# AdaLN block on one core: the B matrices by batch in column groups, with the loads at a stage's start in another order

## The reference

```python
logits = _rms(x, norm_pre_w) @ compete_w.T + compete_b        # 16 slots per batch
vals, idx = top_k(swapaxes(logits, 1, 2), 4)
wgt = softmax(vals, axis=-1)
wx = x @ write_w.T + write_b
gathered = take_along_axis(wx[:, None], idx[..., None], axis=2)
written = einsum('bsk,bskd->bsd', wgt, gathered)
ws = _rms(ws + written, norm_post_w)
q  = (x @ wq.T + bq).reshape(B, L, H, 64)                     # H = 16 heads
kk = (ws @ wk.T + bk).reshape(B, S, H, 64)
vv = (ws @ wv.T + bv).reshape(B, S, H, 64)
att = softmax(einsum('blhd,bshd->bhls', q, kk) / 8, axis=-1)
ctx = einsum('bhls,bshd->blhd', att, vv).reshape(B, L, 1024)
x = _rms(x + ctx @ out_proj_w.T + out_proj_b, norm_post_w)
```

## Time and profile before

| | |
|---|---|
| median of 3 runs | 1112.16 us (1110.51 to 1112.85) |
| profiled execution | 1110.51 us, span 1108.7 us |
| PE busy | 1022.6 us (92%) |
| PEld busy | 579.1 us (52%) |
| DVE busy | 763.4 us (69%) |
| ACT busy | 590.7 us (53%) |
| POOL busy | 459.3 us (41%) |
| DMA | 232.38 MB, mean 210 GB/s |

### The profile page before, as it was taken

How to read it: one execution, slowest core, us unless ns; L and a number is a source line. 1 busy time by engine, 2 the same in 40 slices (tenths; PEclk the granted TensorE clock), 3 DMA queues, 4 the chain that set the end, 5 groups by cost and what they waited for, 6 DMA issues and landing times. The chain is left out here.

```text
span 1108.7 us, 14369 instructions
## 1 busy us (share of the span) xinstructions
PE 1022.6 (92%) x4784; PEld 579.1 (52%) x4784; DVE 763.4 (69%) x1024; ACT 590.7 (53%) x977; POOL 459.3 (41%) x212
## 2 busy tenths in 40 slices
PE   2999999999999968989999999998789899999996
PEld 1344444444444432746666666665327566666663
DVE  4999999999999922365555555554315666666664
ACT  3778878878788630245555555556204333333333
POOL 6899899899999620001111111111100033333333
PEclk9999999999999998999999999999699999999998
DMA  4356555565555469954556576443797666868664
GB/s 137 133 181 199 171 182 179 176 203 163 183 186 171 133 209 411 338 171 158 184 195 229 187 232 213 171 171 127 268 409 279 189 208 215 298 222 294 231 227 151
DMA packets 122143, 232.38 MB, mean 210 GB/s; under 512 B 8163, under 2 KB 83043, under 8 KB 119013
## 3 DMA queue, kind: packets, MB, share of 16 engines
q1 hardware_dynamic: 121444, 229.54, 60.1%
q0 software_dynamic: 640, 2.10, 0.6%
HBM read 139.32 MB, written 92.28 MB: 209 GB/s over the span
## 5 line engine op out<-in xcount | busy, mean ns | idle before, releaser
L966 PE MATMUL bank<-work 128*128 128x256 f32 (+1 forms) x1024 | 244.4, 382 | 8.1 <-PEq L555 5.0
L995 PE MATMUL bank<-work 128*128 128x512 f32 (+1 forms) x512 | 230.3, 592 | 2.1 <-ACT work L1097 1.3
L416 PE MATMUL bank<-work,ident 128*128 128x512 f32 x384 | 190.9, 620 | 40.3 <-DVE work L338 39.6
L966 PEld LDWEIGHTS bank<-work 128*128 128x128 f32 x1024 | 187.2, 190 | 45.2 <-issue 25.3
L1157 POOL TENSOR_TENSOR work<-work 128x1024 f32<-128x1024 f32 x32 | 75.5, 2359 | 237.3 <-DVE work L1079 237.3
L1147 POOL COPY xres<-work 128x1024 f32<-128x1024 f32 x32 | 33.4, 1043 | 332.7 <-DVE work L1079 332.7
L995 PEld LDWEIGHTS bank<-work 128*128 128x128 f32 x512 | 97.1, 190 | 97.6 <-issue 91.8
L416 PEld LDWEIGHTS bank<-work,ident 128*128 128x128 f32 x384 | 65.9, 190 | 146.4 <-issue 99.2
L1030 DVE TENSOR_TENSOR work<-bank,sbias 128x256 f32<-128x256 f32 x64 | 27.2, 424 | 151.4 <-PE bank L966 151.4
L416 PE MATMUL bank<-work 128*128 128x511 f32 x256 | 121.1, 596 | 0.0
L330 DVE SCALAR_TENSOR_TENSOR work<-work,decay 128x512 f32<-128x512 f32 x128 | 120.7, 962 | 0.0
(11 more groups left out here) (153 smaller groups left out, 1437.5 us busy)
## 6 DMA issues: line engine op xcount, KB each, us to landing
work<-in_kT SPq DMA_DIRECT2D x32, 512.0 KB, 3.3
work<-in_xT SPq DMA_DIRECT2D x32, 512.0 KB, 3.9
x0T_scratch<-work SPq DMA_DIRECT2D x32, 512.0 KB, 3.5
x_natural_scratch<-xres SPq DMA_DIRECT2D x32, 512.0 KB, 5.0
work<-x0T_scratch SPq DMA_DIRECT2D x32, 512.0 KB, 4.3
x_natural_scratch<-work SPq DMA_DIRECT2D x32, 512.0 KB, 3.0
x1T_scratch<-work SPq DMA_DIRECT2D x32, 512.0 KB, 2.7
work<-x1T_scratch SPq DMA_DIRECT2D x32, 512.0 KB, 4.9
```

What stands on the lines that cost most here:

```text
L416: return nc.tensor.matmul(ps[:, at:at + n], w, v, start=start, stop=not start, skip_group_check=True)
L966: last = nc.tensor.matmul(ps_s[p], xTb[p][:, c, :], Amat[:, i, :, c * 32:c * 32 + 32], start=(c == 0), stop=(c == NC - 1))
L995: last = nc.tensor.matmul(ps_o[:, cols], attT[:, k * P:(k + 1) * P], Bmat[k][:, i, cols], start=(k == 0), stop=(k == 1), skip_group_check= ...
```

## The change

Everything is in the head, but for the names of the semaphores that the tail waits for.

- B by batch. There are 8 groups, one for each half k of the heads and each batch b, in the order of `groups`. A group has 4 pairs of heads, whose 32 rows go to the 4 column groups of the array (8 matmuls with outputs of 32 rows by 512 columns, one for each pair and half of the columns). The rows come out where `Bmat` and `Bm_d` have them, so a group is evicted in one instruction of 128 x 1024. VectorE evicts groups 0 to 3 and ScalarE groups 4 to 7.
- The output bias is added as VectorE evicts groups 0 to 3 (the first half of the heads), from a buffer `obias` in which 16 rows hold the bias and the rest is zero. GpSimd clears it behind its gathers. The matmuls with K = 1 and their row vectors `head0_row` are gone.
- TensorE starts the groups when VectorE has evicted product 7. Groups 0 and 4 each wait for two quarters of wo_T. A group waits for the eviction of the group three before it, whose bank it takes. Groups (0,2), (0,3) and (1,3) share one staging buffer, so group 3 waits for the write of group 0, and group 5 for that of group 3.
- The 8 score-bias matmuls go to four column groups, in two sets, with one copy of 128 x 256.
- SP sends both wr_T pieces first. Then it waits for the last gather, and sends the write bias and the workspace, the first wk_T piece, the norm weights and the output bias.

```diff
-            step(nc.vector.memset(head0_row[0], 0.0))
...
+        stageB = {(0, 2): cut(8192, 1024), (0, 3): cut(8192, 1024), (1, 2): cut(2048, 1024), (1, 3): cut(8192, 1024)}
+        groups = [(0, 2), (0, 0), (0, 1), (0, 3), (1, 2), (1, 3), (1, 0), (1, 1)]
...
                     piece(0, wr_T, 0)
+                    piece(1, wr_T, 1)
+                    sp.wait_ge(g_in[K - 1], 16)
+                    for h in range(2):
+                        half = slice(CH * h, CH * h + CH)
+                        sp.dma_start(wbb[64 * h:64 * h + 64, :], wr_b[half].rearrange("(o c) -> o c", o=1)
+                                     .broadcast_to([BS, CH])).then_inc(c_in, 16)
+                        if t == 0:
+                            sp.dma_start(ws[64 * h:64 * h + 64, :], work_t[:, half]).then_inc(c_in, 16)
+                    piece(2, wk_T, 0)
                     if t == 0:
...
-                    sp.wait_ge(g_in[K - 1], 16)
-                    piece(1, wr_T, 1)
-                    piece(2, wk_T, 0)
+                        sp.dma_start(npb, npost.rearrange("(o c) -> o c", o=1).broadcast_to([P, C])).then_inc(np_in, 16)
+                    sp.wait_ge(ob_zero, 1)
+                    sp.dma_start(obias[0:S, :], wo_b.rearrange("(o c) -> o c", o=1).broadcast_to([S, C])).then_inc(ob_in, 16)
...
+                    for g, (k, b) in enumerate(groups):
+                        if b >= 2:
+                            wait_group(sp, g)
+                            sp.dma_start(Bm_d[b, k, :, :], stageB[k, b]).then_inc(b_out[t][k, b], 16)
+                        if g == 3:
                             load_bias(sp, t, 1)
+                            sp.wait_ge(grp_ps, 4)
                             load_x(sp, t, 0, 0, 0, 0)
...
-                        r0 = 32 * (hp // 4)
-                        last = nc.tensor.matmul(psK[r0:r0 + 1, hp % 4 * P:(hp % 4 + 1) * P], bqc[:, hp:hp + 1],
-                                                kkz[:, hp, :, :], start=True, stop=True)
+                        r0 = 32 * (hp % 4)
+                        last = nc.tensor.matmul(psK[r0:r0 + 1, hp // 4 * P:(hp // 4 + 1) * P], bqc[:, hp:hp + 1],
+                                                kkz[:, hp, :, :], start=True, stop=True, skip_group_check=True)
...
+                    pe.wait_ge(vv_ok, 4)
+                    pe.wait_ge(sb_ok, 1)
+                    wait_product(pe, HP - 1)
+                    for g, (k, b) in enumerate(groups):
+                        if g % 4 == 0:
+                            for i in range(2):
+                                pe.wait_ge(wo_in[2 * k + i], 16)
+                        wait_group(pe, g - 3)
+                        for h in range(2):
+                            cols = slice(CH * h, CH * h + CH)
+                            for j in range(4):
+                                last = nc.tensor.matmul(group_bank(g)[32 * j:32 * j + 32, cols],
+                                                        vvz[:, 4 * k + j, b, :], ring[k][:, j, cols],
+                                                        start=True, stop=True, skip_group_check=True)
+                        last.then_inc(grp_ps, 1)
+                    wait_product(pe, HP - 2)
+                    keep_warm(banks[0], 3)
...
+                    nc.gpsimd.memset(obias[:], 0.0).then_inc(ob_zero, 1)
...
+                    for g in range(4, 8):
+                        nc.scalar.activation(group_home(act, g), group_bank(g)[:, :], ACT.Copy).then_inc(grp_a, 1)
...
+                    dve.wait_ge(ob_in, 16)
+                    for g in range(4):
+                        nc.vector.tensor_tensor(group_home(dve, g), group_bank(g)[:, :], obias[:], ALU.add)\
+                            .then_inc(grp_d, 1)
```

More of the change, by code:

```diff
@@ L82, in build @@
         rows = sb("rows", [P, P])
[L83 removed]
+        ones_row = rows[0:1, :]
         tiny = sb("tiny", [P, 4])
@@ L510, in load_x @@
             sp.dma_start(xTb[p], src).then_inc(xT_in[t][p], 16)
-        b_out = [[sem(f"B_out_{t}_{i}") for i in range(4)] for t in range(2)]
-        def slot_of(i):
-            k = i - HP
-            return (k % 2, k // 2) if k < 6 else (k % 4, 0)
+        b_out = [{g: sem(f"B_out_{t}_{g[0]}_{g[1]}") for g in stageB} for t in range(2)]
         def head(t):
@@ L540, in prod, with wait_product, group_bank, wait_group @@
             def prod(i):
[L542 to L544 removed]
+                return banks[(0, 3)[i % 2]]
+            def wait_product(eng, i):
                 if i >= 0:
[L547 to L548 removed]
+                    eng.wait_ge(ev_d if i % 2 else ev_a, 2 * (i // 2 + 1))
+            def group_bank(g):
+                return banks[1 + g % 3]
+            def wait_group(eng, g):
+                if g >= 4:
+                    eng.wait_ge(grp_a, g - 3)
+                elif g >= 0:
+                    eng.wait_ge(grp_d, g + 1)
             def keep_warm(ps, n):
@@ L703, in _ @@
-                    wait_product(pe, 2 * HP - 4)
-                    keep_warm(prod(2 * HP - 4), 3)
+                    for hp in range(HP):
+                        ps = prod(hp)
+                        wait_product(pe, hp - 2)
+                        if hp % 4 == 0:
+                            pe.wait_ge(w_in[hp // 4], 16 * 3)
+                        for c in range(NC):
+                            last = nc.tensor.matmul(ps[:, c * P:(c + 1) * P],
+                                                    ring[hp // 4][:, hp % 4, c * P:(c + 1) * P], kkz[:, hp, :, :],
+                                                    start=True, stop=True)
+                        last.then_inc(prod_ps, 1)
@@ L709, in copy_product, with group_home @@
                     done, ps = ev_d if i % 2 else ev_a, prod(i)
[L710 to L729 removed]
+                    new = ps[:, :].rearrange("p (c b r) -> p b c r", c=NC, b=B)
+                    copy(Amat[:, :, i, :].rearrange("p b (c r) -> p b c r", c=NC), new[:, 0:2, :, :])\
+                        .then_inc(done, 1)
+                    wait(eng, st_a[i % 4], 16 * (i // 4))
+                    copy(stageA[i % 4].rearrange("p (b c r) -> p b c r", b=2, c=NC), new[:, 2:B, :, :])\
+                        .then_inc(done, 1)
+                def group_home(eng, g):
+                    k, b = groups[g]
+                    eng.wait_ge(grp_ps, g + 1)
+                    if b < 2:
+                        if k == 0:
+                            for j in (2 * b, 2 * b + 1):
+                                eng.wait_ge(st_a[j], 16 * 2)
+                        return Bmat[k][:, b, :]
+                    if (k, b) == (0, 3):
+                        eng.wait_ge(b_out[t][0, 2], 16)
+                    if (k, b) == (1, 3):
+                        eng.wait_ge(b_out[t][0, 3], 16)
+                    return stageB[k, b]
                 @block.gpsimd
@@ L870, in wait_Bm @@
             def wait_Bm(eng):
-                for k in range(4):
-                    eng.wait_ge(b_out[t][k], 32 * (3, 3, 1, 1)[k])
+                for g in b_out[t]:
+                    eng.wait_ge(b_out[t][g], 16)
             ps_s = [banks[0][:, 0:256], banks[0][:, 512:768]]
```

100 lines of the change are left out of this document (16 added, 84 removed).

## The result

The changed kernel takes 1115.55 us (median of 12 runs, 1112.32 to 1117.08) beside 1112.1 us for the kernel before on the same chip: a ratio of 1.0029, interval 1.0018 to 1.0041. It is slower by 0.3%, where 1102.7 us was forecast. The profiled execution took 1115.01 us with a span of 1113.1 us, 4.4 us more than before.

The account below looks back on a forecast made before the run. PE was taken as busy nearly throughout except in the two heads. Gains of 4.1 (first head) and 4.15 (second) made 8.25 us off 1110.5, 1102.2, set 0.5 higher at 1102.7 us; range 1097.5 to 1108.5, likeliest case 1100 to 1105.

Parts of the forecast that it names:

- 4.15: Second head's loads: the 2.45 us wait for wv_T and 1.7 us of slow clock both go.
- The gathers' delay: Second head: the second wr_T piece goes before the gathers, so PE's transposes come 3.8 us later (ends 0 and 4.4).
- the score bias: Each head: products in four column groups let the transposes start earlier, gain 0.4 us (ends 0 and 1.1).
- The 1.7 us of slow clock: Second head, behind the wait for wv_T: 32 matmuls taking 5.34 us return to 3.64.
- I take a gain of 2.4: First head's loads: the stream is 2.4 us shorter, leaving some 0.3 of PE's 2.74 us of waits.
- The last write lands at 865.3: Second head's B stage: last B write lands then, next tile's load at 868.7, before PE's own end at 869.7.
- Forecast gains 1.6 and 3.4: B stage: us gained in the first and second head, the first after 0.6 taken off for the clock.
- the free biases at the write product: Write bias and workspace loads behind the gathers cost nothing, covered by the 10.04 us write product.
- rival 3: B groups: four column groups with different moving operands don't run together, 3.6 us a group, time 1128; chance 0.04.
- Rival 1: Loads: gathers share the engines with the second piece, delayed 0.5 instead of 3.8 us, time 1099.4; chance 0.14.
- Rival 2: B stage: a falling clock takes its gain, -1.1 and 0.0 for 1.6 and 3.4, time 1108.8 (half: 1105); chance 0.20.
- The premise that a tail keeps whatever it gains at its start: Tails: an earlier start is kept in full, since PE has no gaps inside a tail.

Follow-up runs that it names:

- order_only: The kernel before with only the changed kernel's new order of loads: 1114.66 us, ratio 1.0024.
- wr_half: The changed kernel with the second wr_T piece cut to half its columns, leaving out part of the computation: 1112.43 us, one run.
- groups_only: The changed kernel with the order of loads of before, keeping the B groups and score bias: 1111.13 us, ratio 1.0003.
- mixed: no_warm with the second wr_T piece moved forward in the first head only, the small loads between it and the gathers: ratio 0.9981.
- wr_behind: The changed kernel with the second wr_T piece behind the gathers again, the small loads staying behind them too: ratio 1.0036.
- wo_half: The changed kernel with wo_T loads cut to 512 of 1024 columns, leaving out part of the computation: 1106.0 us, one run.
- staging: The changed kernel with groups (0,3) and (1,3) in the other staging buffer, so only groups 4 and 5 wait for a write: 1112.08 us, ratio 1.0001.
- no_warm: The changed kernel with the order of loads of before and groups (0,3) and (1,3) in the other staging buffer: 1109.22 us, ratio 0.9968.
- split: no_warm with the changed kernel's order of loads in the first head only: 1108.37 us, ratio 0.9968.

## Why the prediction was wrong

The error is 12.65 us on the span: 8.25 forecast as a gain, 4.4 lost. By the traces 6.4 of it lie in the B stage, 2.55 in the loads of the second head, 1.9 in those of the first, and 1.8 in the first tail. So no step alone turned the sign: the loads are a loss by themselves (order_only), and the B stage, which was to give 5.0 and would have covered it, lost 1.4. The forecast also took its sum off the fastest of three runs and gave back only 0.5 of the 1.65 us to the median. By its own steps:

**First: "4.15" for the loads in the second head: a gain that did not come.** The gathers' delay was right: transposes at +16.04, 3.81 later where 3.8 was forecast. The gain set against it was not. From the transposes to the A products it took 32.99 us, before 35.00: 2.0 less, where 4.15 and 0.4 for the score bias were forecast. Even the 2.0 is mostly the clock's: in the five other kernels with the old order in this head it took 32.5 to 33.9 us (mean 33.1), and in the five with the new order and the groups 32.3 to 33.6 (mean 32.7). So the loads gave some 0.4 us for a delay of 3.8. Two things stand behind that.

The stream isn't a matter of bytes alone. The reasoning took 2.10 MB off it and counted 5.0 us. But behind the gathers SP may send only what has a free slot: one wk_T piece. The next waits for half of the write product, which waits for the gathers. Ten microseconds from about where SP's wait for the last gather ends, after:

```profile
801.00:806.00 5.00, 2.70 (x12) 1.11 (x16) 3.31 (x5) 0.00 (x0) 0.00 (x0) 0.50 0.63 206
806.00:811.00 5.00, 5.00 (x40) 1.31 (x36) 1.05 (x2) 0.00 (x0) 0.00 (x0) 0.78 0.76 300
```

Before, the same ten:

```profile
796.00:801.00 5.00, 3.06 (x16) 1.01 (x20) 3.77 (x6) 0.00 (x0) 0.00 (x0) 0.68 0.87 311
801.00:806.00 5.00, 5.00 (x36) 1.24 (x32) 0.23 (x1) 0.00 (x0) 0.00 (x0) 0.64 0.99 423
```

That is 2.53 MB for 3.67 MB: of the 2.10 MB saved, 1.14 are lost to an idle queue. SP's own rows show it, the second wk_T piece going out 7.6 us after the first:

```profile
802.41 0.59 SPq L563 DMA_DIRECT2D work<-in_wk_T  x1
...
809.99 0.34 SPq L563 DMA_DIRECT2D work<-in_wk_T  x1
```

In wr_half the gathers come 2.5 us earlier and the A products only 1.0 earlier, but 1.3 us is what they scatter by among the kernels with this order, so that run doesn't decide it. That slots and not something else hold it is read from these rows; no run with more slots was made.

The 1.7 us of slow clock in the earlier trace rows were one execution's. None of the five other traces with the old order in this head has it. groups_only has the same loads, and waits that add to 3.1 us, but keeps its clock:

```profile
814.70 3.64 PE L633 MATMUL bank<-work 128*32 128x512 f32 x32 [1.20 <-DMA work<-in_wk_T]
819.61 3.64 PE L633 MATMUL bank<-work 128*32 128x512 f32 x32 [1.27 <-DMA work<-in_wv_T]
824.50 3.64 PE L633 MATMUL bank<-work 128*32 128x512 f32 x32 [0.66 <-DMA work<-in_wv_T]
```

Over all kernels the A products start at 44.9 to 47.2 with the old order in this head, and at 48.0 to 49.6 with the new one. The means are 2.8 us apart, which agrees with order_only's loss (1114.66 less 1111.8).

**Second: "I take a gain of 2.4" for the first head: mis-sized.** Some 0.3 us of waiting was to remain, and 2.26 did (1.74 and 0.52). A products start at 49.57 for 50.20: 0.6, where 2.4 - 0.3 + 0.4 were forecast, and between 49.5 and 51.1 in all kernels with the new order there, 50.2 to 51.3 with the old (mixed and wr_behind apart). The piece saves some 4.5 us (wr_behind against after), but the small loads behind the gathers, which were to cost 2.6, cost 3.9 (wr_behind against before), or 4.3 with the score bias's 0.4. Both differences rest on single traces.

**Third: "The last write lands at 865.3", and the end put on TensorE's own path: the step of the B stage that failed, and the largest part of the error.** Forecast gains 1.6 and 3.4; from the A products to the next tile it took 42.06 and 42.04 us, before 41.67 and 40.99: losses of 0.4 and 1.05. The waits at VectorE's fourth add and ScalarE's second copy were in the forecast and came:

```profile
862.74 1.22 DVE L840 TENSOR_TENSOR work<-bank,lgT 128x1024 f32<-128x1024 f32 x1 [1.70 <-DMA B_scratch<-work]
866.97 2.85 ACT L768 ACTIVATE work<-bank 128x1024 f32<-128x1024 f32 x3 [2.69 <-DMA B_scratch<-work]
```

The write between them took 2.89 us, as forecast, though it is one of 512 KB and the row it was taken from one of 128 KB. It is the last write that took 5.78 us and not 2.9 (5.9 in the first head). SP had sent the write of group (1,2) and the load of a tail tile ahead of it in both. In the second head, counted from the start of the A products, group 0 started 1.6 us late, the fourth add 2.1, and the last write landed 38.4 us on, where 33.2 was forecast. The forecast put PE's own end (869.7) after the load behind the writes (868.7), and it was the other way round. In the first head the chain up to group 4 came as forecast (the fourth add at +26.8 in both). Groups 4 to 7 then ran at a fallen clock, 8.77 us for 7.07, of which the forecast had taken off 0.6, and the last write did the rest. With the staging taken apart the stage takes 39.3 and 40.5 us, which is a gain of 2.4 and 0.5, less the 0.9 that the tail takes back.

**Fourth: wo_T before group 0: not in the forecast.** It was looked for only before group 4. There the first head has it as forecast (2.02 us for 2.1; wo_half, with half the bytes, has none), and in the second the groups found it already there. Group 0 needs two quarters at once, and waited for them, 2.97 us in the second head, of which the copy of the last A product sets 1.5. The earlier trace rows had landings of up to 7.4 and 9.1 us; after, they take 5.6 to 9.4.

Right were the score bias (16 records in 0.62 us, about 0.4 us gained), the column groups (rival 3 is out: four different moving operands run together), the gathers' delay, and the free biases at the write product. Rival 1 is out. Rival 2 is there in part: 3.50 us for what takes 1.77 in the second head's B stage, 8.77 for 7.07 in the first. In the second head it isn't what held the next tile up, since in staging that wait goes although the clock falls all the same; in the first it has a part. With the writes out of the way it costs: with the staging taken apart, the second head's stage takes 40.5 us with a fallen clock (staging) and 39.0 to 39.7 without (no_warm, mixed, split, which have the old order of loads as well).

The premise that a tail keeps whatever it gains at its start is off by about 0.9 us where the next tile comes at once, as read at staging.

The Trainium skill, "DMA: Bandwidth & Descriptors", section "Queues, rings and completion order", has each DMA engine take turns between its queues. Over the longer overlaps that the trace of before could not show, the traces still disagree: from 790 to 795 us after, while the four gathers were issued (789.61 to 793.40), it was

```profile
q1 hardware_dynamic: 138, 2.00, 93.6%
q0 software_dynamic: 23, 0.09, 4.6%
```

## What to carry to other kernels

Before moving a load forward, ask three things of the trace: what is issued behind it on another queue while it is still under way (here a gather, on which everything hung), which loads could use the room that it leaves (none, where a ring's slots are full), and how long a wait for a store becomes when loads are in its queue. Fewer instructions gain nothing where a write that frees a shared buffer ends the stage: take the buffers apart first. And a slow clock that stands in one trace isn't a gain to count.

## What was not expected of the hardware

- A gather issued beside queued bulk loads got almost nothing: 23 packets in 5 us beside 138 of the hardware queue, and none in mixed from 407.55 to 412. It landed 3.5 us after its issue with the queue nearly empty, and up to 9.2 us with it full (staging). The delay went by the bytes ahead: taking 1.05 MB out brought the transposes 2.5 us forward (wr_half).
- The length of a wait did not tell whether TensorE's clock falls behind it. It fell after 1.33 us in the tail (767.16), and not after 1.34 us at the same place of the kernel before. It fell after 2.08 and 2.21 us, and not after 3.07 us in wr_behind's first head. After a wait of 3.32 us for wv_T it held in staging's second head and fell in wr_half's. A fall costs 1.3 to 1.7 us at these places.
